# A two-layer network on one Trainium2 core: other orders of work at the opening of the state-space part

## The chip, the cores and the metric

The kernel runs on one core of one Trainium2 chip. Its time is the device time of one execution in microseconds (us). Five engines work side by side, each through its own queue in order: TensorE (PE) multiplies and transposes, ScalarE (ACT) applies functions and copies, VectorE (DVE) does elementwise arithmetic, GpSimd (POOL) does some more of it, and SyncE (SP) issues the DMA loads. They wait for each other by semaphores only.

## What is computed

The reference applies six blocks, each on a layer normalisation of `x` (4 x 256 tokens of width 512) and each added to it. The fifth is the state-space block (Mamba 2, 128 heads of 64, 8 groups, chunks of 128 tokens), whose opening is changed:

```python
proj = hidden_states @ in_proj_w.T
gate, xBC, dt = jnp.split(proj, [INTER, INTER + CONV_DIM], axis=-1)
# causal convolution of width 4 over xBC, then silu; split into x, Bm, Cm
dt = jnp.clip(jax.nn.softplus(dt + dt_bias), DT_MIN, DT_MAX)
cs = jnp.cumsum(dA, axis=-1)                       # dA = dt * A, in each chunk
Lmat = jnp.where(tri, jnp.exp(seg), 0.0)           # seg = cs[l] - cs[s]
xdt = xc * dtc[..., None]
scores = jnp.einsum('bclhn,bcshn->bchls', Cc, Bc) * Lmat
Ydiag = jnp.einsum('bchls,bcshp->bclhp', scores, xdt)
# Yoff: the first chunk's state for the second; then y * silu(gate), group norm, out projection
```

## The kernel before

All products are in float32 by three passes: each operand is split into a rounded high part and the rest (`...h`, `...l`), and `product` (L1815) runs high x high, high x low, low x high, 4 matmuls of 512 columns each, 12 for a chunk. A weight tile is loaded by SyncE into `rawA` (six slots), ScalarE makes the high part (`hi_A`, L719), GpSimd the rest (`lo_A`, L576) in place of the raw tile, and only then TensorE may use it. `A0G + i` is the i-th input-projection tile of the state-space part; chunk `c` of a group is half `c % 2` (512 tokens) of tile `c // 2`. Tiles 0 and 1 give B and C, even tiles from 2 on give x, odd ones the gate. All but the gate pass through the convolution (`conv_start` and `conv_silu` on ScalarE, three `taps` on VectorE between them); the gate takes `gate_silu`.

Each engine's order at the opening is written out by hand, and these orders are what is changed. `x` is normalised tile by tile for the new block: TensorE transposes a tile (`layer_transpose`), ScalarE copies it to `xTh` (`layer_hi`, L687), VectorE makes `xTl` (`layer_lo`, L1207), which raises `ln_lo`. TensorE runs dt_product(0), chunks 2, 4 and 6 of group 0 with the transposes of tiles 4, 5, 6 and 7 between and behind them, then waits for `ln_lo` of tile 7 and runs dt_product(1), dt_transpose(0), chunk 1, sums(0), chunk 3, the transposed sums, dt_transpose(1), chunk 5, sums(1), chunk 7, and the products of B and C.

ScalarE makes `dt` in four activations for each half of the tokens (`dt_act(p, 0)` to `dt_act(p, 3)`: bias, absolute value, exponential, logarithm; a change between exponential, logarithm and silu brings a table load), copies it token-wise (`dt_tokens`, L1073), copies the running sums (`running_sums`, L1078), and later turns the loaded rows into decays: `spans` (eight activations), then `first_exp`. SyncE's `first_rows(p)` (L446) waits for running_sums(p), writes them to memory, waits for that write and loads them back, broadcast, into `eb`; behind `first_rows(0)` in its queue stands the load of tile `A0G + 5`.

On VectorE, `scale_x(v, g, p)` scales x by dt for half p of step v and `decay_off` and `decay` (L1555) multiply the decays by the products of B and C; `decay` raises `m_s`. TensorE's `y_products(v, g, p)` (the pair products of a step; each half is one) needs `m_s` and `m_xdt`. A group has four steps v; a step on TensorE is two chunks, `y_products` of both halves, further chunks, and the transposes for the next step. GpSimd's `step` begins with the `lo_A` of the tiles that the step loads, then the squares for the norm.

Of the kernel before, what the change touches and what calls it, by code (L numbers as in the profile page):

```python
# [16 lines left out]
KC = D // P  # L17
# [30 lines left out]
def build(nc, x_in, w0_in, b0_in, lb_in, wqkv_in, wo_in, fa_in, fb_in, ma_in, mb_in, dtw_in, chp_in, cst_in, out):  # L48
# [228 lines left out]
    A0G = A0M + 1  # L277
# [72 lines left out]
    def step_tiles(v, last):  # L350

        if v < TPG - 2:
            return [2 + 2 * (v + 2), 3 + 2 * (v + 2)]
        if last:
            return []
        return [NA_G + i for i in (range(4) if v == TPG - 2 else (4, 5))]
# [129 lines left out]
    def _(pool):  # L486
# [150 lines left out]
                                    ALU.pow).then_inc(m_rstd, 1)  # L637

        def step(v, g, last=False, first=False):
            for i in step_tiles(v, last):  # L640
                lo_A(A0G + i, g, NA_G)
            if last and v == TPG - 2:
                for u in range(4):
                    lo_A(A0F + u)
            if v % 2 == 1:
                lo_B(B0G + v + 1, g, TPG)
                lo_B(B0G + v + 2, g, TPG)
            if v == 0 and not first:
                rstd_of(g - 1)
            if last and v == TPG - 2:  # L650
                pool.wait_ge(m_s, 2 * NG * TPG)
            square(v, g, 0)
            square(v, g, 1)
# [32 lines left out]
    def _(act):  # L686
        def layer_hi(k, t, bank):  # L687
            act.wait_ge(ln_tp, 8 * k + t + 1)
            nc.scalar.activation(xTh[:, :, t * P:(t + 1) * P], ps[:, bank, :].rearrange("p (k t) -> p k t", k=KC),  # L689
                                 ACT.Copy).then_inc(ln_hi, 1)  # L690
# [225 lines left out]
        def conv_start(g, c, slot):  # L916

            n = conv_index(g, c)
            act.wait_ge(m_in, chunk_count(g, c))
            if n >= 6:  # L920
                act.wait_ge(m_conv, n - 1)
            elif n == 5:
                act.wait_ge(ln_tp, 40)
            nc.scalar.activation(conv_acc(g, c), ps[:, chunk_bank(g, c), :], ACT.Identity,  # L924
                                 bias=param(slot, c // 2, 4),
                                 scale=param(slot, c // 2, 3)).then_inc(m_acc, 1)
# [190 lines left out]
        dt_act(0, 2)  # L1117
        conv_start(0, 2, 1)
        layer_hi(4, 6, 4)
        layer_hi(4, 7, 5)  # L1120
        dt_act(0, 3)
        conv_start(0, 4, 1)
        hi_B(B0G)
        hi_B(B0G + 1)
# [5 lines left out]
        dt_act(1, 3)  # L1130
        conv_start(0, 1, 1)
        conv_start(0, 3, 1)
        dt_tokens(1)
        token_sums(0)
        conv_silu(0, 0)
# [14 lines left out]
        first_exp(0)  # L1150
        spans(0, 0, 1)
        first_exp(1)
        hi_A(A0G + 5)
        act.wait_ge(m_csf, 2)
        nc.scalar.activation(erow[:, :, :], csf[:, 1:NT:2, :], ACT.Exp).then_inc(m_erow, 1)
        act.sem_inc(m_par, 4)
# [15 lines left out]
    def _(dve):  # L1172
# [615 lines left out]
        end_weights(1)  # L1788
        dve.wait_ge(m_wdt, 2)
        scale_x(0, 0, 0)  # L1790
        scale_x(0, 0, 1)
        decay_off(0, 0, 0)
        decay(0, 0, 0)
        decay_off(0, 0, 1)
        decay(0, 0, 1)
        step(0, 0, first=True)
# [14 lines left out]
    def _(pe):  # L1811
        def mm(o, l, r, start, end, **kw):
            return nc.tensor.matmul(o, l, r, start=start, stop=end, **kw)  # L1813

        def product(o, lh, ll, rh, rl, start=True, end=True, **kw):  # L1815

            passes = [(a, b) for l, r in ((lh, rh), (lh, rl), (ll, rh)) for a, b in zip(l, r)]
            for n, (a, b) in enumerate(passes):
                last = mm(o, a, b, start and n == 0, end and n == len(passes) - 1, **kw)
            return last  # L1820

# [332 lines left out]
                                       m % NF == 0, m % NF == NF - 1)  # L2154
                    last.then_inc(m_out, 1)

        def in_chunk(g, c):

            tile, half = c // 2, c % 2
            n = A0G + tile  # L2160
            pe.wait_ge(A_lo, g * NA_G + n + 1)
            if g == 0 and c < 8:
                bank = chunk_bank(g, c)
                if c == 0:
                    pe.wait_ge(f_h, 2 * NF - 1)
                elif c == 2:
                    pe.wait_ge(f_g, 2 * NF)
                elif c == 6:
                    pe.wait_ge(m_dts, 1)
                elif c % 2:  # L2170
                    pe.wait_ge(ln_lo, 40)
                    pe.wait_ge(m_tap, 3 * {1: 0, 3: 1, 5: 2, 7: 3}[c] + 3)
            else:
                p = c - 3
                gp = g if p >= 0 else g - 1
                p = p % GCH
                ptile = p // 2
                if ptile < 2 or ptile % 2 == 0:
                    k = p if ptile < 2 else 4 + (ptile - 2) // 2 * 2 + p % 2
                    pe.wait_ge(m_tap, 3 * (gp * XCH + k) + 3)  # L2180
                else:
                    pe.wait_ge(m_gate, gp * 2 * TPG + (ptile - 3) // 2 * 2 + p % 2 + 1 + (g == 0 and c == 9))
            wh, wl = wA(n)
            cols = slice(512 * half, 512 * half + 512)
            return product(ps[:, chunk_bank(g, c), :], wh, wl, [xTh[:, kc, cols] for kc in range(KC)],
                           [xTl[:, kc, cols] for kc in range(KC)])

        def chunk(g, c):
            in_chunk(g, c).then_inc(m_in, 1)

        def bc(g, b):

# [199 lines left out]
        layer_transpose(4, 4, 4, False)  # L2392
        chunk(0, 4)
        layer_transpose(4, 5, 5, False)
        chunk(0, 6)
        layer_transpose(4, 6, 4, False)
        layer_transpose(4, 7, 5, False)
        pe.wait_ge(x_new, XB[4] + NT)
        pe.wait_ge(ln_lo, 40)
        dt_product(1)  # L2400
# [119 lines left out]
```

## Time and profile before

| | |
|---|---|
| median of 3 runs | 2123.57 us (2123.4 to 2125.83) |
| profiled execution | 2123.11 us, its span 2121.3 us |
| TensorE matmul busy | 2082.7 us (98%) |
| VectorE busy | 1649.1 us (78%) |
| ScalarE busy | 1432.3 us (68%) |
| GpSimd busy | 1055.2 us (50%) |
| mean granted TensorE clock | 0.998 |

The span runs from the first to the last instruction. Busy shares are means over the whole span; the stretch of the change, about 500 to 562 us, is read by itself. A timeline merges equal instructions that follow each other: "x8" behind a line says that there are eight, and its length is that of all of them. An engine's instructions overlap slightly, so that the next can start before the last has ended. The idle time in brackets is that just before the line, and behind the arrow stands what ended it.

### The profile page before, as it was taken

What the parts mean: (1) busy time and instruction counts of PE and PEld (TensorE: products, weight loads), DVE (VectorE), ACT (ScalarE), POOL (GpSimd) and SP (SyncE); (2) the same over time, 40 slices, a digit from 0 to 9 for tenths busy, and PEclk for the clock granted to TensorE, in tenths of its full rate; (3) what the DMA queues carried; (4) which work ended last, traced back from release to release, by engine and by line L of the source; (5) the groups of instructions that cost most, each with busy time, mean ns of one, the idle gap of its engine ahead of it and who ended that gap; (6) DMA issues with size and microseconds to landing.
All of it is one profiled execution on the core that took longest, in us unless ns stands there. A gap on an engine that the chain in (4) does not pass through costs nothing.

```text
span 2121.3 us, 34818 instructions
## 1 busy us (share of the span) xinstructions
PE 2082.7 (98%) x12586; PEld 1730.0 (82%) x12596; DVE 1649.1 (78%) x2675; ACT 1432.3 (68%) x3090; POOL 1055.2 (50%) x758
## 2 busy tenths in 40 slices
PE   8999999999999999999999999999999999999999
PEld 7866698888788888888888888888888888888887
DVE  7777773325889998898898999889889889998222
ACT  5498743335978777778777877777877787783332
POOL 6577545452355356354455535535445553555452
PEclk9999999999999999999999999999999999999999
DMA  3000013332433233233224323323322432232332
GB/s 139 1 1 2 1 60 95 95 90 71 139 136 124 78 121 116 83 130 140 90 90 140 131 77 111 124 79 126 139 90 90 140 137 81 102 115 60 95 95 84
DMA packets 65337, 202.53 MB, mean 95 GB/s; under 512 B 7056, under 2 KB 9104, under 8 KB 56976
## 3 DMA queue, kind: packets, MB, share of 16 engines
q1 hardware_dynamic: 65168, 200.31, 27.9%
q8 instruction: 102, 1.67, 0.3%
q14 instruction: 67, 0.55, 0.1%
HBM read 197.39 MB, written 2.88 MB: 94 GB/s over the span
## 4 chain that ended last, share of the span: by engine, by line
PE 92%; ACT 3%; DVE 3%; issue 1%; DMA 0%; POOL 0%; DVEq 0%; SPq 0%; ACTq 0%; POOLq 0%
PE ps L1813 86%; PE ps L2211 3%; PE ps L1998 2%; PE ps L1828 1%; ACT eb L961 0%; DVE bst L1187 0%; ACT xTh L689 0%; DVE xTl L1210 0%; PE ps L2266 0%; ACT pr_a L828 0%; DVE PT L1417 0%; DVE rs L1362 0%; ACT pr_b L828 0%; DMA cst<-cst_in 0%; DVE eb L1561 0%
## 5 line engine op out<-in xcount | busy, mean ns | idle before, releaser
L580 POOL TENSOR_TENSOR wAl<-rawA,wAh 128x512 fp32r<-128x512 f32 x233 | 343.8, 1490 | 362.4 <-ACT wAh L722 362.0
L1813 PE MATMUL ps<-xTh,wAh 128*128 128x512 f32 (+1 forms) x1528 | 418.8, 396 | 3.9 <-DVE xTl L1210 3.9
L1813 PE MATMUL ps<-xTl,wAh 128*128 128x512 f32 (+1 forms) x1528 | 405.8, 387 | 0.0
L1813 PE MATMUL ps<-xTh,wAl 128*128 128x512 f32 (+1 forms) x1528 | 405.3, 387 | 0.0
L1515 DVE SCALAR_TENSOR_TENSOR work<-ps,chp,work 128x510 f32<-128x510 f32 (+2 forms) x465 | 343.4, 744 | 22.7 <-ACT work L924 12.7
L1813 PEld LDWEIGHTS ps<-xTl,wAh 128*128 128x128 f32 x1528 | 285.2, 188 | 60.1
L1813 PEld LDWEIGHTS ps<-xTh,wAl 128*128 128x128 f32 x1528 | 285.3, 188 | 58.7
L586 POOL TENSOR_TENSOR wBl<-rawB,wBh 128x512 fp32r<-128x512 f32 x108 | 139.7, 1307 | 388.0 <-ACT wBh L726 388.0
L1813 PEld LDWEIGHTS ps<-xTh,wAh 128*128 128x128 f32 x1528 | 277.1, 188 | 66.4 <-issue 12.8
L961 ACT ACTIVATE eb<-eb,gc 128x128 f32<-128x128 f32 x1008 | 307.6, 392 | 0.0
L924 ACT ACTIVATE work<-ps,gpar 128x512 f32<-128x512 f32 x155 | 119.4, 771 | 128.8 <-PE ps L1813 96.9
L630 POOL TENSOR_TENSOR sqt<-gt 128x512 f32<-128x512 f32 x110 | 167.4, 1522 | 69.6 <-DVE gt L1577 55.4
L1469 DVE TENSOR_TENSOR hs<-ps,gs 128x512 f32<-128x512 f32 x44 | 30.4, 691 | 202.1 <-PE ps L1813 167.1
L1561 DVE TENSOR_TENSOR eb<-eb,cbD 128x1024 f32<-128x1024 f32 x128 | 184.1, 1477 | 0.0
L632 POOL TENSOR_TENSOR sq<-sq,sqt 128x512 f32<-128x512 f32 x110 | 178.2, 1620 | 8.6
L1813 PE MATMUL ps<-eb,xdt 128*64 128x128 f32 x2048 | 159.6, 277 | 5.0 <-DVE eb L1561 5.0
L1813 PE MATMUL ps<-wBh,yTh 128*128 128x512 f32 x512 | 162.3, 397 | 0.0
L1813 PE MATMUL ps<-wBl,yTh 128*128 128x512 f32 x512 | 159.3, 391 | 0.0
L1813 PE MATMUL ps<-wBh,yTl 128*128 128x512 f32 x512 | 159.1, 391 | 0.0
L722 ACT ACTIVATE wAh<-rawA 128x512 fp32r<-128x512 f32 x233 | 142.2, 620 | 21.0 <-DMA rawA<-fa_in 19.4
L948 ACT ACTIVATE gt<-ps 128x512 f32<-128x512 f32 x128 | 75.7, 591 | 118.4 <-PE ps L1813 118.4
L1583 DVE SCALAR_TENSOR_TENSOR yTl<-gt,chp,yTh 128x512 fp32r<-128x512 f32 x128 | 122.1, 954 | 39.3 <-ACT yTh L975 39.1
(213 smaller groups left out, 3958.6 us busy)
## 6 DMA issues: line engine op xcount, KB each, us to landing
eb<-scr_decays SPq DMA_DIRECT2D x62, 1536.0 KB, 6.5
rawA<-ma_in SPq DMA_DIRECT2D x144, 256.0 KB, 6.8
rawA<-fa_in SPq DMA_DIRECT2D x88, 256.0 KB, 2.6
rawB<-mb_in SPq DMA_DIRECT2D x64, 256.0 KB, 2.8
rawB<-fb_in SPq DMA_DIRECT2D x44, 256.0 KB, 2.6
x<-x_in SPq DMA_DIRECT2D x8, 256.0 KB, 6.3
x_out<-x SPq DMA_DIRECT2D x8, 256.0 KB, 2.7
wqraw<-wqkv_in SPq DMA_DIRECT2D x1, 1536.0 KB, 10.7
```

What stands on the lines that cost most here:

```text
L580: nc.gpsimd.tensor_tensor(wAl[:, slot, :], rawA[:, slot, :], wAh[:, slot, :].bitcast(F32), ALU.subtract).then_inc(A_lo, 1)
L586: nc.gpsimd.tensor_tensor(wBl[:, slot, :], rawB[:, slot, :], wBh[:, slot, :].bitcast(F32), ALU.subtract).then_inc(B_lo, 1)
L630: nc.gpsimd.tensor_tensor(sqt[:, :], y, y, ALU.mult).then_inc(m_sqt, 1)
L632: nc.gpsimd.tensor_tensor(sq[:, half], sq[:, half], sqt[:, :], ALU.add).then_inc(m_sq, 1)
L722: nc.scalar.activation(wAh[:, n % SLOTA, :], rawA[:, n % SLOTA, :], ACT.Copy).then_inc(A_hi, 1)
L924: nc.scalar.activation(conv_acc(g, c), ps[:, chunk_bank(g, c), :], ACT.Identity, bias=param(slot, c // 2, 4), scale=param(slot, c // 2, 3) ...
L948: nc.scalar.activation(gt[:, v % 2, 512 * (c % 2):512 * (c % 2) + 512], ps[:, chunk_bank(g, c), :], ACT.Silu).then_inc(m_gate, 1)
L961: last = nc.scalar.activation(eb[:, v % 2, h, t, :], eb[:, v % 2, h, t, :], ACT.Relu, bias=start, scale=-1.0)
L1515: nc.vector.scalar_tensor_tensor(out=acc[:, :, j:S], in0=src[:, :, 0:S - j], scalar=param(g, c // 2, 3 - j), in1=acc[:, :, j:S], op0=ALU.m ...
L1561: nc.vector.tensor_tensor(e, e, w.unsqueeze(1).to_broadcast([P, 2, 4 * P]), ALU.mult).then_inc(m_s, 1)
L1583: nc.vector.scalar_tensor_tensor(out=yTl[:, v % 2, half], in0=gt[:, v % 2, half], scalar=param(g, 2 + 2 * v, 6), in1=yTh[:, v % 2, half].b ...
L1813: return nc.tensor.matmul(o, l, r, start=start, stop=end, **kw)
```

## The change

It alters the order of work at five places and no arithmetic.

- TensorE: the transposes of tiles 6 and 7, which stood behind chunk 6, are issued inside it, ahead of its matmuls 2 and 10 (counted from 0). `product` gets an argument `between` for this.
- ScalarE: `dt_act(0, 3)`, the logarithm of the first half, moves from behind the copy of tile 7 to ahead of it.
- ScalarE: `hi_A(A0G + 5)`, the high part of tile 5, moves from behind the last `first_exp` to ahead of `dt_tokens(1)`.
- VectorE: `scale_x(0, 0, 1)` moves behind the first half's `decay_off` and `decay`.
- GpSimd: at steps 0 and 1 of group 0 it waits for both halves' decays of that step (`m_s`) before the splits.

```diff
--- before.py
+++ after.py
@@ -637,6 +637,8 @@
                                     ALU.pow).then_inc(m_rstd, 1)
 
         def step(v, g, last=False, first=False):
+            if g == 0 and v < 2:
+                pool.wait_ge(m_s, 2 * v + 2)
             for i in step_tiles(v, last):
                 lo_A(A0G + i, g, NA_G)
             if last and v == TPG - 2:
@@ -1117,8 +1119,8 @@
         dt_act(0, 2)
         conv_start(0, 2, 1)
         layer_hi(4, 6, 4)
+        dt_act(0, 3)
         layer_hi(4, 7, 5)
-        dt_act(0, 3)
         conv_start(0, 4, 1)
         hi_B(B0G)
         hi_B(B0G + 1)
@@ -1130,6 +1132,7 @@
         dt_act(1, 3)
         conv_start(0, 1, 1)
         conv_start(0, 3, 1)
+        hi_A(A0G + 5)
         dt_tokens(1)
         token_sums(0)
         conv_silu(0, 0)
@@ -1150,7 +1153,6 @@
         first_exp(0)
         spans(0, 0, 1)
         first_exp(1)
-        hi_A(A0G + 5)
         act.wait_ge(m_csf, 2)
         nc.scalar.activation(erow[:, :, :], csf[:, 1:NT:2, :], ACT.Exp).then_inc(m_erow, 1)
         act.sem_inc(m_par, 4)
@@ -1788,9 +1790,9 @@
         end_weights(1)
         dve.wait_ge(m_wdt, 2)
         scale_x(0, 0, 0)
-        scale_x(0, 0, 1)
         decay_off(0, 0, 0)
         decay(0, 0, 0)
+        scale_x(0, 0, 1)
         decay_off(0, 0, 1)
         decay(0, 0, 1)
         step(0, 0, first=True)
@@ -1812,10 +1814,12 @@
         def mm(o, l, r, start, end, **kw):
             return nc.tensor.matmul(o, l, r, start=start, stop=end, **kw)
 
-        def product(o, lh, ll, rh, rl, start=True, end=True, **kw):
+        def product(o, lh, ll, rh, rl, start=True, end=True, between={}, **kw):
 
             passes = [(a, b) for l, r in ((lh, rh), (lh, rl), (ll, rh)) for a, b in zip(l, r)]
             for n, (a, b) in enumerate(passes):
+                if n in between:
+                    between[n]()
                 last = mm(o, a, b, start and n == 0, end and n == len(passes) - 1, **kw)
             return last
 
@@ -2154,7 +2158,7 @@
                                        m % NF == 0, m % NF == NF - 1)
                     last.then_inc(m_out, 1)
 
-        def in_chunk(g, c):
+        def in_chunk(g, c, between={}):
 
             tile, half = c // 2, c % 2
             n = A0G + tile
@@ -2183,10 +2187,10 @@
             wh, wl = wA(n)
             cols = slice(512 * half, 512 * half + 512)
             return product(ps[:, chunk_bank(g, c), :], wh, wl, [xTh[:, kc, cols] for kc in range(KC)],
-                           [xTl[:, kc, cols] for kc in range(KC)])
-
-        def chunk(g, c):
-            in_chunk(g, c).then_inc(m_in, 1)
+                           [xTl[:, kc, cols] for kc in range(KC)], between=between)
+
+        def chunk(g, c, between={}):
+            in_chunk(g, c, between).then_inc(m_in, 1)
 
         def bc(g, b):
 
@@ -2392,9 +2396,7 @@
         layer_transpose(4, 4, 4, False)
         chunk(0, 4)
         layer_transpose(4, 5, 5, False)
-        chunk(0, 6)
-        layer_transpose(4, 6, 4, False)
-        layer_transpose(4, 7, 5, False)
+        chunk(0, 6, {2: lambda: layer_transpose(4, 6, 4, False), 10: lambda: layer_transpose(4, 7, 5, False)})
         pe.wait_ge(x_new, XB[4] + NT)
         pe.wait_ge(ln_lo, 40)
         dt_product(1)
```

## Rows read from the trace of the kernel before

**Rows 1.** The page, part 1, first line: busy us (share of span) xinstructions.
```profile
PE 2082.7 (98%) x12586; PEld 1730.0 (82%) x12596; DVE 1649.1 (78%) x2675; ACT 1432.3 (68%) x3090; POOL 1055.2 (50%) x758
```

**Rows 2.** Chain that ended last, 499 to 572 us: start us, length us, what.
```profile
509.15 1.30 DVE xTl L1210 x2
...
540.57 0.52 ACT wAh L722
...
558.62 3.37 DVE eb L1561 x2
...
562.03 7.22 PE ps L1813 x48
```

**Rows 3.** Waits of TensorE, whole span: us in total, times, longest us.
```profile
PE ps L1813 <- DVE eb L1561: 5.0, 4, 2.2
```

**Rows 4.** Timeline of ScalarE: start us, length us, instruction, [idle before <-releaser].
```profile
508.52 1.08 ACT L689 ACTIVATE xTh<-ps 128x512 fp32r<-128x512 f32 x2
509.62 1.28 ACT L1071 ACT_TABLE_LOAD   x1
510.91 0.63 ACT L1071 ACTIVATE dts<-dts 128x512 f32<-128x512 f32 x1
511.45 0.76 ACT L924 ACTIVATE sqt<-ps,gpar 128x512 f32<-128x512 f32 x1
...
514.03 0.60 ACT L1075 ACTIVATE dtt<-ps 128x512 f32<-128x512 f32 x1 [0.78 <-PE ps L2363]
...
520.16 1.52 ACT L924 ACTIVATE gt<-ps,gpar 128x512 f32<-128x512 f32 x2
522.25 0.60 ACT L1075 ACTIVATE dtt<-ps 128x512 f32<-128x512 f32 x1 [0.57 <-PE ps L2363]
...
529.94 0.62 ACT L1085 ACTIVATE ctok<-ps 128x512 f32<-128x512 f32 x1
```

**Rows 5.** Timeline of TensorE, 496 to 572 us, columns as in rows 4.
```profile
510.58 1.16 PE L1813 MATMUL ps<-xTh,wAh 128*128 128x512 f32 x4 [1.67 <-DVE xTl L1210]
...
539.86 0.66 PE L1813 MATMUL ps<-eb,xdt 128*64 128x128 f32 x8 [1.08 <-DVE eb L1561]
...
543.62 1.12 PE L1813 MATMUL ps<-eb,xdt 128*64 128x128 f32 x8 [2.22 <-DVE eb L1561]
...
559.81 0.66 PE L1813 MATMUL ps<-eb,xdt 128*64 128x128 f32 x8 [1.04 <-DVE eb L1561]
...
562.03 0.66 PE L1813 MATMUL ps<-eb,xdt 128*64 128x128 f32 x8 [0.69 <-DVE eb L1561]
```

**Rows 6.** Slices of 1 us: busy time and count of each engine, then granted clock.
```profile
543.00:544.00 1.00, 0.39 (x4) 0.39 (x6) 1.00 (x2) 1.00 (x4) 1.00 (x1) 0.83 0.17 62
...
545.00:546.00 1.00, 1.00 (x12) 1.00 (x10) 0.75 (x2) 1.00 (x4) 0.00 (x0) 0.50 0.00 0
...
547.00:548.00 1.00, 1.00 (x6) 0.82 (x5) 0.93 (x3) 1.00 (x5) 1.00 (x1) 0.97 0.79 197
```

**Rows 7.** Timeline of SyncE's DMA issues: start us, length us, issue.
```profile
518.34 0.33 SPq L450 DMA_DIRECT2D scr_decays<-csf  x1
...
521.81 1.41 SPq L388 DMA_DIRECT2D rawA<-ma_in  x3
```

**Rows 8.** Line 388's landings: its issue at 521.81, then all five to 560.
```profile
DMA to landing us min/median/max: 5.2/5.2/5.2
...
DMA to landing us min/median/max: 5.2/5.5/6.9
```

**Rows 9.** The page, part 6: issue, count, KB each, median us to landing.
```profile
rawA<-fa_in SPq DMA_DIRECT2D x88, 256.0 KB, 2.6
```

**Rows 10.** Line 1561, step 0's two decays: duration ns min/median/max, start us.
```profile
L1561 DVE TENSOR_TENSOR eb<-eb,cbD x1: 1219/1219/1219, 538.6 to 538.6; 128x1024 f32<-128x1024 f32 x1
...
L1561 DVE TENSOR_TENSOR eb<-eb,cbD x1: 2289/2289/2289, 541.3 to 541.3; 128x1024 f32<-128x1024 f32 x1
```

**Rows 11.** Timeline of GpSimd, 496 to 572 us, columns as in rows 4.
```profile
541.17 3.52 POOL L580 TENSOR_TENSOR wAl<-rawA,wAh 128x512 fp32r<-128x512 f32 x2 [25.81 <-ACT wAh L722]
```

## The prediction

> **What bounds the kernel now.** I read four views in this order. The page's totals say that TensorE is busy for 98% of the span [rows 1], so the kernel is TensorE-bound almost everywhere and an edit pays or costs only where TensorE stands idle. The chain that ended last, read between 499 and 572 us, shows where that is: up to 505 us and again from 562.03 us the chain is TensorE's own, and between the two it runs mostly through ScalarE, with pieces of VectorE and one of TensorE from 510.58 to 514 [rows 2]. The waits view of TensorE agrees: its four waits for VectorE's decays, 5.0 us in all, all lie in this stretch [rows 3], and from 562.03 on it has no further one for them. So the quantity to forecast is one time stamp: when the second pair product of step 1 starts, now at 562.03 us. Whatever it shifts by, the end shifts by.
>
> The ScalarE timeline then says how full that engine is. Between 514.03 and 558 us it has one idle time of note, 0.57 us ahead of the second copy to `dtt` [rows 4]. Hence in this stretch a conversion moved from one place of ScalarE's queue to another is worth nothing by itself; every microsecond that ScalarE waits is worth a microsecond at 562. The TensorE timeline gives the idle times that are the result: 1.67 us before dt_product(1), 2.22 before the second pair product of step 0, 0.69 before the one of step 1 [rows 5].
>
> **Edit 1: the last two transposes inside chunk 6.** The same 8 transposes and 12 matmuls run, so TensorE's work is unchanged. The transposes of tile 6 now end near 506 us instead of near 508.3. Nobody uses that: ScalarE's copy of tile 6 starts at 508.52 directly behind `conv_start(0, 2)`, without idle time [rows 4]. Their own waits (`ln_norm`, `ln_lo`) are met: VectorE has nothing left before tile 6's rest but that copy. Value 0. The cover is ScalarE's queue; if it were empty, up to the 1.67 us of idle before dt_product(1) could be won.
>
> **Edit 2: dt_act(0, 3) between the copies of tiles 6 and 7.** This adds something to the path. Now the two copies take 1.08 together, then come the table load of 1.28 and the logarithm of 0.63 [rows 4]. After the edit: copy of tile 6 from 508.52 to 509.12 (a copy of this size takes 0.60, as those to `dtt`); load 509.14 to 510.42; logarithm from 510.43; the copy of tile 7 can start 0.54 after it (the pitch of the next instruction behind the logarithm at 510.91, whose neighbour starts at 511.45), so 510.97 to 511.57. VectorE's rest of tile 7 now starts at 509.75 (the pair takes 1.30 from 509.15 [rows 2], the last 0.69 of it is tile 7's); it will start at 511.59. That is +1.84, and dt_product(1), now at 510.58 [rows 5], waits for exactly this. Behind it in TensorE's queue stands dt_transpose(0), and on that waits dt_tokens(0), for which ScalarE already idles 0.78 us now [rows 4]. So that idle time grows to 2.62 us and all of ScalarE's later stream moves by **+1.84**. What is won, the logarithm 0.48 earlier, feeds dt_clip(0), which on VectorE stands behind the rest of tile 7 anyway. The Trainium skill, page "ScalarE: Activation LUTs", section "What ACT_TABLE_LOAD costs", adds about 1.38 us of drain to each switch of set; by it the copy of tile 7 would be later still and the term +3.2. The row shows the logarithm 0.01 us behind the 1.28 us load, so the trace does not agree and I keep its number.
>
> **TensorE's clock.** TensorE's idle time before dt_product(1) becomes 1.67 + 1.84 = 3.5 us. The nearest rows: after idle times of 1.08 and 2.22 us, with about 1.5 us of work between, the granted clock is 0.83 in the slice from 543 us, 0.50 (1.2 instead of 2.4 GHz) in those up to 547 and 0.97 in the next, and the first 8 matmuls take 1.12 where the same take 0.66 at full clock; behind the 1.67 us before dt_product(1) the first four take 1.16, which is full speed [rows 5, 6]. The slices hold 0.17 + 3 + 0.03 = 3.3 to 3.4 us at half clock in all, which costs half of it, 1.7 us. The new idle time is longer than the one that was followed by the lower clock, so I take **+1.70**; the ends are 0 and 1.70. It falls on dt_product(1) and dt_transpose(0), which ScalarE waits for, so nothing covers it.
>
> **Edit 3: hi_A(A0G + 5) behind conv_start(0, 3).** This is the large term. ScalarE ends the two `conv_start` at 521.68 [rows 4] and would then wait for the load of that tile. SyncE issues this load behind `first_rows(0)`: the write of the running sums at 518.34, its completion, three broadcasts, and then, at 521.81, the tile [rows 7]. The issue itself comes after ScalarE has arrived. The load lands 5.2 us later [rows 8], at 527.0. Both ends hang on running_sums(0), so edit 2 moves both alike and the gap stays. In ScalarE's queue behind the waiting conversion stand dt_tokens(1), token_sums(0), the convolution's activations and running_sums(1): all that the critical stretch consists of. The conversion starts at 527.05 and takes 0.52 of the queue, so dt_tokens(1) starts at 527.57 instead of 522.25: **+5.32** (the idle 0.57 is thereby used up). TensorE's sums(1) wait for this through VectorE. TensorE then stands about 4 us idle; should its clock fall there too, chunk 7 and its transposes end 7.65 us after dt_tokens(1), and ScalarE wants them 7.69 after (now 529.94 less 522.25 [rows 4]). It just fits: 0, with an upper end of +1.7.
> Bounds of the landing: the five loads of this line in the stretch take 5.2 to 6.9 us, the same size in the SwiGLU stage 2.6 by the page's median [rows 8, 9]. I take 5.2, the very load. The Trainium skill, page "DMA: Bandwidth & Descriptors", section "Anatomy of one DMA — SWDGE (gpsimd) path", gives 2.0 us plus the bytes over 436 GB/s, 2.6 us for 256 KB; by it the term would be +2.7 and the sum 5.0. The section is about another issuing path, and the row disagrees.
> At its old place the conversion is gone: `erow` and all that follows it on ScalarE come 0.52 earlier (its piece of the chain is 0.52 long [rows 2]): **-0.52**.
>
> **Edit 4: the decays ahead of the second scaling.** Decay 0 of step 0 no longer waits for scale_x(0, 0, 1), some 0.93 us, which moves into VectorE's idle time before the second half (it waits for the exponentials till 540.57). The first pair product of step 0 comes up to 0.9 earlier, and this is worth nothing: the second one and ScalarE's stream set what follows. If that idle time were missing, 0.93 would be lost.
>
> **Edit 5: GpSimd waits for the decays.** VectorE's decay of 128x1024 takes 1.22 us alone and 2.29 beside GpSimd's splits; the split beside it runs long as well, two splits taking 3.52 [rows 10, 11]. In step 0 the second decay ends 1.07 earlier; it feeds a pair product behind which TensorE waits again, 1.04 us at 559.81 [rows 5], so it doesn't reach 562. In step 1 the second decay is again disturbed (the two take 3.37 where 2.44 would be undisturbed [rows 2]); undisturbed it ends about 1 earlier, and the pair product starts when TensorE is free, 0.69 earlier [rows 5]: **-0.69**. The added wait queues two splits and the squares behind it on GpSimd. The splits move by 1 to 2 us, and are wanted by chunks more than 10 us away; cost 0.
>
> **Sum.** 1.84 + 1.70 + 5.32 - 0.52 - 0.69 = +7.65 us. The profiled execution took 2123.11 us (span 2121.3 and 1.8 around it), the median is 2123.57. I forecast 2130.8 for a like execution and 2131.2 for the median. A measurement of this kernel can tell about 0.2%, 4.2 us, from no change.
>
> **Rivals.**
> (a) TensorE's clock stays up over 3.5 us of idle time. For it: it stayed at 1.00 over 1.67 us. Sum 5.95, 2129.5. Chance 0.17.
> (b) The second idle time brings a lower clock that isn't covered (the margin is 0.04 us): 7.65 + 1.7, 2132.9. Chance 0.11.
> (c) The load lands in 2.6 us as in the SwiGLU stage: 5.05, 2128.6; with (a) 3.35, 2126.9, which counts as no change. Chance 0.09.
> (d) The other side: ScalarE doesn't wait at the moved conversion, because the tile is there. Then its 0.52 fits into the idle 0.57, and 1.84 + 1.70 - 1.21 = +2.3 is left, 2125.9: no change. The point from which it decides is a wait below 1.9 us, a landing by 523.6. Against it: the issue stands at 521.81 and hangs on the same queue. Chance 0.06.
> (e) As (d), and the logarithm's place costs nothing either: only -1.21 is left, 2122.4. Against it: no idle time lies between the copies. Chance 0.03.
> The forecast has 0.54.
>
> **Range.** (a) and the forecast span 5.95 to 7.65; (b) and the upper landing of 6.9 reach 9.35, with the spread of the runs before (up to 2.3 over the median) 2134; (c) reaches down to 2127. So 2127.0 to 2134.0. Slower by over 0.2%: forecast, (a), (b) and most of (c), 0.88; within: 0.11; faster 0.01.
>
> **What would show it.** Right: a ScalarE idle time of about 5.3 us ended by a DMA into `rawA` behind the second `conv_start` to `gt`; the idle time before the first `dtt` at 2.6 or 4.3 us; TensorE idle 3.5 us before dt_product(1), with a granted clock of 0.50 behind it; decays of 1.22 us; the second pair product of step 1 at 569.7. Wrong: the conversion without idle time, or dt_product(1) at 510.6; or TensorE with new idle time behind 570 us, for a split of step 1 that comes too late.

## The result

The changed kernel takes 2134.2 us (median of 6 runs, 2131.54 to 2135.98); the kernel before, beside it, 2123.55. The ratio is 1.0046, with a 95% interval of 1.0036 to 1.0056: slower, clear of noise. In a later set of runs beside the kernel before it took 2131.28 (5 runs, 2130.56 to 2134.99) against 2123.46, a ratio of 1.0038 (1.0025 to 1.0052). The forecast was 2131.2 and slower; the first median lies 0.2 us above the upper end of the stated range (2134.0), the second inside it, and the first ratio times the median before, 2133.3, too. The profiled execution took 2131.54 us with a span of 2129.4, 8.1 us more than before.

Busy times are those of before: TensorE 2083.5 us of matmuls, ScalarE 1432.0, VectorE 1648.6, GpSimd 1053.3. The loss is for the most part idle time of TensorE, and all of it stands in the opening. ScalarE's timeline of the changed kernel (columns as in rows 4):

```profile
508.43 0.59 ACT L691 ACTIVATE xTh<-ps 128x512 fp32r<-128x512 f32 x1
509.04 1.28 ACT L1073 ACT_TABLE_LOAD   x1
510.33 0.63 ACT L1073 ACTIVATE dts<-dts 128x512 f32<-128x512 f32 x1
510.87 0.58 ACT L691 ACTIVATE xTh<-ps 128x512 fp32r<-128x512 f32 x1
...
517.37 0.60 ACT L1077 ACTIVATE dtt<-ps 128x512 f32<-128x512 f32 x1 [4.21 <-PE ps L2367]
...
523.49 1.51 ACT L926 ACTIVATE gt<-ps,gpar 128x512 f32<-128x512 f32 x2
530.74 0.63 ACT L724 ACTIVATE wAh<-rawA 128x512 fp32r<-128x512 f32 x1 [5.75 <-DMA rawA<-ma_in]
531.27 0.58 ACT L1077 ACTIVATE dtt<-ps 128x512 f32<-128x512 f32 x1
...
539.74 0.60 ACT L1087 ACTIVATE ctok<-ps 128x512 f32<-128x512 f32 x1 [0.61 <-PE ps L2389]
```

Where [rows 4] had two copies side by side at 508.52, the table load and the logarithm stand between them now. The first copy to `dtt` has 4.21 us of idle time ahead of it (0.78 before), and the moved conversion (`wAh`) 5.75, ended by the DMA into `rawA`; the second copy to `dtt` is behind it. New is also the 0.61 ahead of `ctok`, which followed without idle time before. TensorE's timeline shows the same from its side:

```profile
505.04 0.71 PE L1815 MATMUL ps<-xTh,wAh 128*128 128x512 f32 x2
...
512.32 1.66 PE L1815 MATMUL ps<-xTh,wAh 128*128 128x512 f32 x4 [3.39 <-DVE xTl L1212]
513.77 1.91 PE L1815 MATMUL ps<-xTl,wAh 128*128 128x512 f32 x4
515.48 1.41 PE L1815 MATMUL ps<-xTh,wAl 128*128 128x512 f32 x4
...
533.31 2.07 PE L1815 MATMUL ps<-cst,dA 128*128 128x128 f32 x8 [5.03 <-DVE dA L1746]
...
569.10 0.66 PE L1815 MATMUL ps<-eb,xdt 128*64 128x128 f32 x8 [1.91 <-DVE eb L1563]
...
570.46 0.61 PE L1815 MATMUL ps<-eb,xdt 128*64 128x128 f32 x8
```

dt_product(1) starts at 512.32 behind 3.39 us of idle time (1.67 in [rows 5]), and its three passes take 1.66, 1.91 and 1.41 us, where they took 1.16, 1.07 and 1.07 before. The group at 570.46 is the second pair product of step 1 (569.10 is the first): the time stamp that the prediction followed, 562.03 before [rows 2, 5]. It now follows without idle time. The granted clock, in slices of 2 us (clock behind the counts):

```profile
509.00:511.00 2.00, 0.00 (x0) 0.00 (x0) 0.69 (x1) 1.97 (x4) 0.00 (x0) 1.00 0.00 0
...
513.00:515.00 2.00, 2.00 (x6) 1.57 (x5) 1.96 (x3) 0.15 (x1) 2.00 (x2) 0.50 0.00 0
515.00:517.00 2.00, 2.00 (x9) 1.58 (x8) 1.46 (x2) 0.00 (x0) 0.42 (x1) 0.71 0.00 0
...
533.00:535.00 2.00, 1.69 (x8) 1.69 (x9) 1.93 (x4) 1.99 (x4) 0.00 (x0) 0.56 0.00 0
```

Executions start the opening up to 1.1 us later or 0.2 earlier. So from here on the stamp is counted from the start of chunk 6 (505.05 before, 505.04 after): **56.98 us before, 65.42 after, +8.44.** What comes behind it is the same work in all kernels here. These stamps, and all stamps below, come from one profiled execution of each kernel.

### The profile page after: what moved, and what is told of

It reads as the page before. It is cut to its first block, busy times and chain, and to the rows that moved or that the text cites. A ratio compares the mean times of both kernels' runs of the same rounds, so it can differ in the third digit from the quotient of the medians.

```text
span 2129.4 us, 34830 instructions
## 1 busy us (share of the span) xinstructions
PE 2083.5 (98%) x12596; PEld 1729.5 (81%) x12596; DVE 1648.6 (77%) x2675; ACT 1432.0 (67%) x3090; POOL 1053.3 (49%) x758
## 3 DMA queue, kind: packets, MB, share of 16 engines
q8 instruction: 102, 1.67, 0.3%
## 4 chain that ended last, share of the span: by engine, by line
PE 92%; DVE 3%; ACT 3%; issue 1%; DMA 1%; SPq 0%; POOL 0%; DVEq 0%; ACTq 0%
PE ps L1815 86%; PE ps L2215 3%; PE ps L2002 2%; PE ps L1832 1%; ACT eb L963 0%; DVE bst L1189 0%; DMA lb_raw<-lb_in 0%; PE ps L2270 0%; ACT pr_a L830 0%; ACT xTh L691 0%; DVE xTl L1212 0%; DMA rawA<-ma_in 0%; DVE PT L1419 0%; DVE rs L1364 0%; ACT pr_b L830 0%
```

## The experiments

Each kernel ran beside the kernel before, whose median was 2123.42 to 2123.85 us in these sets; the ratio is to those runs, and not the quotient of two medians of the table. "Stamp" is the second pair product of step 1, counted from chunk 6; "tail" what is left of the span behind it; clock 1910 to 1940 is the mean granted clock in that stretch.

| kernel | median us | ratio to before (95%) | wait for the load | stamp | tail | clock 1910 to 1940 |
|---|---|---|---|---|---|---|
| before | 2123.57 | | none | 56.98 | 1559.3 | 0.94 |
| changed | 2134.20 | 1.0046 (1.0036 to 1.0056) | 5.75 | 65.42 | 1558.9 | 1.00 |
| changed, again | 2131.28 | 1.0038 (1.0025 to 1.0052) | 5.21 | 66.73 | 1561.0 | 0.89 |
| conversion back | 2126.18 | 1.0007 (0.9998 to 1.0016) | none | 59.47 | 1558.9 | 1.00 |
| logarithm back | 2130.28 | 1.0027 (1.0018 to 1.0037) | 5.39 | 62.60 | 1562.1 | 0.94 |
| both back | 2123.61 | 0.9997 (0.9987 to 1.0006) | none | 56.04 | 1561.1 | 0.89 |
| load first | 2126.03 | 1.0013 (1.0004 to 1.0022) | none | 58.94 | 1558.8 | 1.00 |
| load in between | 2127.09 | 1.0015 (1.0006 to 1.0024) | 1.27 | 61.25 | 1559.4 | 0.94 |
| first idle time filled | 2129.88 | 1.0030 (1.0019 to 1.0041) | 5.14 | 63.22 | 1558.9 | 1.00 |
| both idle times filled | 2131.96 | 1.0036 (1.0022 to 1.0049) | 6.63 | 65.04 | 1559.2 | 1.00 |
| GpSimd's wait alone | 2124.27 | 1.0004 (0.9995 to 1.0013) | none | 56.10 | 1559.7 | 0.94 |
| scaling order alone | 2123.69 | 0.9999 (0.9990 to 1.0008) | none | 56.98 | 1560.8 | 0.89 |
| load first, logarithm back | 2122.51 | 0.9992 (0.9983 to 1.0001) | none | 55.52 | 1561.0 | 0.89 |
| the same, conv_start(0, 2) late | 2121.83 | 0.9993 (0.9984 to 1.0002) | none | 55.22 | 1559.4 | 0.94 |

**1. The conversion back at its old place.** The changed kernel with

```diff
-        hi_A(A0G + 5)
         dt_tokens(1)
...
         first_exp(1)
+        hi_A(A0G + 5)
```

> The changed kernel with hi_A(A0G + 5) back at its old place behind the last first_exp. Theory W (most of the loss is ScalarE waiting 5.75 us for the load of that tile, with the dt copy behind it in its queue): no ScalarE idle time ended by a DMA here; the second pair product of step 1, at 562.03 us before and 570.46 in the changed kernel, comes at 562.03 + 1.74 + 1.60 - 0.85 = 564.5 us; time about 2126. Rival (the stretch is late for another cause, the logarithm's place and the lower TensorE clock behind it, and the wait only fills time that would be idle): it stays at 569 or later, time 2131 or more.

```profile
517.75 0.60 ACT L1077 ACTIVATE dtt<-ps 128x512 f32<-128x512 f32 x1 [4.22 <-PE ps L2367]
...
525.96 0.60 ACT L1077 ACTIVATE dtt<-ps 128x512 f32<-128x512 f32 x1 [0.60 <-PE ps L2367]
```

The idle time ended by a DMA is gone (timeline of ScalarE), the 4.22 us ahead of the first `dtt` stay. The stamp is 59.47, or +2.49 over before; the theory's sum was 1.74 + 1.60 - 0.85 = 2.49. The conversion's new place, which is the wait and what hung on it, was 5.95 of the 8.44 us.

**2. The logarithm back.** The changed kernel with

```diff
-        dt_act(0, 3)
         layer_hi(4, 7, 5)
+        dt_act(0, 3)
```

> The changed kernel with dt_act(0, 3) back behind the copy of tile 7. Theory L (its place delays dt_product(1) by 1.74 us and the lower clock behind the longer idle time costs 1.60 more): dt_product(1) starts at 510.6 again, the granted clock stays at 1.00 behind it, the first copy to dtt starts at 514.0; the wait for the load stays (about 5.5 us). Second pair product of step 1 at 570.46 - 3.34 = 567.1, time 3.3 us under that of the changed kernel, about 2128 to 2131. Rival (ScalarE absorbs the logarithm, its place is free): the pair product stays at 570.4, time as the changed kernel's.

```profile
514.53 0.60 ACT L1077 ACTIVATE dtt<-ps 128x512 f32<-128x512 f32 x1 [0.77 <-PE ps L2367]
...
527.57 0.63 ACT L724 ACTIVATE wAh<-rawA 128x512 fp32r<-128x512 f32 x1 [5.39 <-DMA rawA<-ma_in]
...
537.53 0.60 ACT L1087 ACTIVATE ctok<-ps 128x512 f32<-128x512 f32 x1 [1.58 <-PE ps L2389]
```

The first `dtt` again has 0.77 us of idle time, and the clock is 1.00 from 509 to 519 us. The stamp fell by 2.82, to 62.60, not by 3.34: the idle time ahead of the second `ctok` is 1.58 us here instead of 0.61. The copy to `dtt` behind the conversion comes 3.77 us earlier here (22.46 us after chunk 6 instead of 26.23), and 0.95 of it is lost again by the second `ctok`. In this execution the mean clock from 525 to 541 us was 0.79, in that of the changed kernel 0.89. The theory holds for the part it was about (first `dtt` 8.89 us after chunk 6, 12.33 in the changed kernel, 8.98 before), and the remainder is a second place that costs.

**3. Both back.** Both edits above in one kernel.

> Both ScalarE edits undone; left are the transposes inside chunk 6, the later second scaling and GpSimd's wait for the decays. Theory: only the gain of undisturbed decays is left, the second pair product of step 1 at 561.2 to 561.4 instead of 562.03, time 2122.7 to 2123.0 against 2123.5. Rival (one of the three other edits has a cost of its own that the large terms hide, such as a late split or a late chunk 6): at 562 or later, time 2123.5 or more.

```profile
505.08 0.71 PE L1815 MATMUL ps<-xTh,wAh 128*128 128x512 f32 x2
...
559.76 0.66 PE L1815 MATMUL ps<-eb,xdt 128*64 128x128 f32 x8 [1.92 <-DVE eb L1563]
...
561.12 0.60 PE L1815 MATMUL ps<-eb,xdt 128*64 128x128 f32 x8
```

TensorE's timeline: the second pair product (561.12) follows without idle time, 56.04 after chunk 6, 0.94 before that of the kernel before. Experiment 8 accounts for 0.88 of it, and no other edit shows a cost of its own. dt_product(1) starts 5.45 us after chunk 6 instead of 5.53, so the earlier transposes are worth 0.08. The median did not move all the same (ratio 0.9997): 0.94 us is 0.04%, and in the profiled execution the clock near 1920 us was lower for longer than in that of before (0.89 against 0.94), and the tail was 1.8 longer.

**4. The load ahead of `first_rows(0)`.** The changed kernel with, on SyncE,

```diff
-        first_rows(0)
         mamba_A(5, 0)
+        first_rows(0)
```

> The changed kernel with SyncE's load of tile A0G + 5 issued ahead of first_rows(0) instead of behind it; ScalarE's order is the changed one. Theory W (the wait comes from the load's place in SyncE's queue): the load is issued as soon as dt_product(1) is done, near 517 us, lands by 522.5 even if it takes 5.6 us, and ScalarE's conversion at 525 finds it there; no idle time ended by a DMA, second pair product of step 1 at 562.03 + 3.34 - 0.54 - 0.85 = 564.0, time about 2125.5. Rival (the load is slow for its own sake or the slot comes free late): an idle time of several us is left and the time stays above 2129.

```profile
518.01 0.33 SPq L388 DMA_DIRECT2D rawA<-ma_in  x1
522.75 0.33 SPq L450 DMA_DIRECT2D scr_decays<-csf  x1
```

SyncE's timeline: the one load is issued at 518.01, 4.7 us ahead of the write of the sums. The landings view of that issue:

```profile
DMA to landing us min/median/max: 2.5/2.5/2.5
```

It took 2.5 us, and ScalarE's conversion at 525.98 followed its `conv_start` without waiting. The stamp is 58.94, +1.96 over before; the expectation's sum was 3.34 - 0.54 - 0.85 = 1.95. So the conversion's new place costs nothing once the load stands elsewhere in SyncE's queue; the stamp is even 0.53 earlier than with the conversion at its old place (59.47 in experiment 1). The 1.96 that are left are the logarithm's place and the clock behind it, less what the other edits gain.

**5. The load in between.** The changed kernel with the same load behind the completion of the write, ahead of the three broadcasts:

```diff
             sp.wait_ge(m_scr, 16 * (p + 1))
+            if p == 0:
+                mamba_A(5, 0)
...
         first_rows(0)
-        mamba_A(5, 0)
```

> The changed kernel with the load of tile A0G + 5 issued inside first_rows(0), behind the completion of the write and ahead of the three broadcast loads. Theory Q (the load takes 5.0 to 6.6 us because three broadcasts of 768 KB in all are in front of it in the same DMA queue; first in the queue it took 2.5): it is issued 3.5 us after the running sums instead of with them in front, lands 2.6 us later, and ScalarE waits 1.3 to 1.5 us instead of 5.75; the second pair product of step 1 comes 60.5 to 61.1 us after the start of chunk 6 (65.42 in the changed kernel, 56.98 before), time 2126.5 to 2128. Rival (the memory traffic of that moment makes it slow, wherever it stands): it takes 5 us again, ScalarE waits about 3.8, the pair product at 63.4.

```profile
518.48 0.60 ACT L1078 ACTIVATE dtt<-ps 128x512 f32<-128x512 f32 x1 [5.30 <-PE ps L2368]
...
527.38 0.63 ACT L725 ACTIVATE wAh<-rawA 128x512 fp32r<-128x512 f32 x1 [1.27 <-DMA rawA<-ma_in]
```

Its landing took 2.6 us, and ScalarE waited 1.27 us (timeline). So it is the place behind the broadcasts that makes it 5.0 to 6.5 us; at the same moment, ahead of them, it is short. Whether the broadcasts hold it up by their order in the queue or by the DMA engines that they occupy is not told apart. The stamp is 61.25, over the expected 60.5 to 61.1. The first `dtt` has 5.30 us of idle time ahead of it, against 4.21 in the changed kernel: 1.09 of the stamp is a longer stretch of low clock (mean 0.66 from 509 to 519 us instead of 0.83). Without it the stamp would be 60.16, now under that range, and next to the 60.21 that experiment 4 plus the wait gives (58.94 + 1.27).

**6. TensorE kept busy ahead of dt_product(1).** The changed kernel with 14 matmuls whose result is overwritten:

```diff
         pe.wait_ge(x_new, XB[4] + NT)
+        for _ in range(14):
+            mm(ps[:, 6, :], wA(A0M)[0][0], xTh[:, 0, 0:512], True, True)
         pe.wait_ge(ln_lo, 40)
```

> The changed kernel with 14 additional matmuls of 512 columns (3.2 us) that TensorE runs in its idle time ahead of dt_product(1), into a bank that dt_product(1) then overwrites. Theory C (1.60 us of the loss is TensorE's clock at half rate behind the longer idle time): granted clock 1.00 from 509 to 525 us, dt_product(1) and its transposes run at full speed, first copy to dtt at 515.8 instead of 517.37, second pair product of step 1 at 568.9 instead of 570.46; median 1 to 2 us under the changed kernel's. Rival (those 1.60 us are a cost of the wait, not of the clock, as a longer first fill): nothing moves.

```profile
509.00:513.00 4.00, 3.89 (x17) 2.90 (x17) 1.68 (x3) 3.97 (x7) 0.00 (x0) 1.00 0.00 0
513.00:517.00 4.00, 4.00 (x21) 3.27 (x21) 3.89 (x6) 1.44 (x4) 2.72 (x2) 1.00 0.00 0
```

The clock stays at 1.00 in both slices, and the first `dtt` comes 10.68 us after chunk 6 instead of 12.33 (516.25 less 505.57): -1.65. The stamp is 63.22, lower by 2.20, since the load took 0.6 less as well (wait 5.14 against 5.75). The 1.60 us were the clock, not the wait itself. The times agree but are weaker evidence: the median is 1.4 us under the later set of the changed kernel, and the intervals of the two ratios overlap.

**7. Both idle times filled.** As 6, and 21 more behind chunk 5, into bank 4, ahead of sums(1). TensorE also waits for the copy of the first running sums ahead of them (`m_csf`), which was done long before.

> As e5_warm1, and 21 more such matmuls (4.8 us) in the idle time ahead of sums(1), where TensorE waits for the second dt copy. Theory C2 (ScalarE's 0.61 us of new idle time ahead of the second token sums is chunk 7 at half clock behind 5.03 us of idle time): that idle time goes, pair product at 568.9 - 0.8 = 568.1 us, no half clock between 509 and 550, and the runs lie closer together than the changed kernel's (2131.5 to 2136.0). Rival (that idle time has another cause, VectorE's dA or the banks): it stays, and the time is e5_warm1's.

```profile
533.15 1.16 PE L1815 MATMUL ps<-cst,dA 128*128 128x128 f32 x8 [1.18 <-DVE dA L1746]
...
568.13 1.03 PE L1815 MATMUL ps<-eb,xdt 128*64 128x128 f32 x8 [1.92 <-DVE eb L1563]
...
569.37 1.07 PE L1815 MATMUL ps<-eb,xdt 128*64 128x128 f32 x8
```

ScalarE's idle time ahead of the second `ctok` is gone, and from the second `dtt` to the first pair product of step 1 it takes 37.0 us (531.1 to 568.13) instead of 37.8 (531.27 to 569.10), as expected. The stamp that the expectation named, the second pair product, comes at 570.65 nevertheless instead of 568.1, and the median is 2131.96 (2130.78 to 2132.21), 2 us over the kernel of 6. Two causes are in its trace: the wait for the load was 6.63 us, 1.49 more than in 6, and the lower clock came at about 568.3 instead, where TensorE sets the end (timeline: a group of 8 takes 1.03 and 1.07 instead of 0.66 and 0.61, and the second pair product follows the first after 2.52 us instead of 1.36). So its five runs do lie closer together, as expected, but not earlier: the mechanism was right, the forecast of the time wrong. Whether the filling itself brought about the later low clock or the slower load is open.

**8. GpSimd's wait alone, in the kernel before.**

```diff
         def step(v, g, last=False, first=False):
+            if g == 0 and v < 2:
+                pool.wait_ge(m_s, 2 * v + 2)
```

> The kernel before with only GpSimd's wait for the decays. Theory: both second decays take 1.22 us instead of 2.29 and 2.30; only step 1's is on the path: second pair product of step 1 at 56.1 to 56.3 us after the start of chunk 6 instead of 56.98, time 0.7 to 0.9 under before. Rival (the gain of the changed kernel there comes from the earlier scaling order or from TensorE's idle time): 56.98 stays.

```profile
538.45 1.22 DVE L1563 TENSOR_TENSOR eb<-eb,cbD 128x1024 f32<-128x1024 f32 x1
...
541.13 2.29 DVE L1563 TENSOR_TENSOR eb<-eb,cbD 128x1024 f32<-128x1024 f32 x1
...
558.40 2.35 DVE L1563 TENSOR_TENSOR eb<-eb,cbD 128x1024 f32<-128x1024 f32 x2
```

```profile
543.48 0.66 PE L1815 MATMUL ps<-eb,xdt 128*64 128x128 f32 x8 [2.23 <-DVE eb L1563]
```

VectorE's timeline: step 1's two decays take 2.35 (3.44 in the kernel before), and the stamp is 56.10, -0.88: all the gain of the change. Step 0's second decay still takes 2.29, since the first split, whose conversion stands at its old place here, has no wait ahead of it; it is not on the path. Against the expectation only one of the two got shorter. TensorE's timeline (the last line) has something else to say: behind 2.23 us of idle time these 8 matmuls take 0.66, full speed, where they took 1.12 behind 2.22 in the kernel before [rows 5]. The time shows no difference (1.0004, 0.9995 to 1.0013).

**9. The scaling order alone, in the kernel before.**

```diff
         scale_x(0, 0, 0)
-        scale_x(0, 0, 1)
         decay_off(0, 0, 0)
         decay(0, 0, 0)
+        scale_x(0, 0, 1)
```

> The kernel before with only scale_x(0, 0, 1) behind the first half's decays. Theory: the first pair product of step 0 starts about 0.9 us earlier, the second one and step 1's stay: 56.98 us after the start of chunk 6, time unchanged within 0.2 us. Rival (the earlier pair product lets TensorE's later chunks and so step 1 start earlier, or the longer idle time between the two pair products brings a lower clock): step 1's second pair product moves by more than 0.3 us.

```profile
538.76 0.66 PE L1813 MATMUL ps<-eb,xdt 128*64 128x128 f32 x8 [0.16 <-DVE eb L1561]
...
543.45 0.66 PE L1813 MATMUL ps<-eb,xdt 128*64 128x128 f32 x8 [3.15 <-DVE eb L1561]
...
561.86 0.66 PE L1813 MATMUL ps<-eb,xdt 128*64 128x128 f32 x8 [0.69 <-DVE eb L1561]
```

TensorE's timeline: the first pair product of step 0 comes at 538.76 and is followed by 3.15 us of idle time instead of 2.22; from there on nothing moves, the stamp is 56.98 to the hundredth.

**10. The load first and the logarithm back.** The rest as changed:

> The changed kernel with the load of tile A0G + 5 ahead of first_rows(0) and the logarithm back behind the copy of tile 7; the early conversion stays. Theory: the conversion now lies in the 0.57 us for which ScalarE waits ahead of the second copy to dtt, so it leaves the full stretch: second pair product of step 1 at 561.13 (both ScalarE edits undone) less 0.52 = 560.6, against 562.03 before; no wait for a DMA; time 2122.0 to 2122.8. Rival (the early conversion brings nothing once it no longer waits, since something else has come last by then): 561.1 as with both undone.

ScalarE's timeline, then TensorE's:

```profile
521.31 0.62 ACT L724 ACTIVATE wAh<-rawA 128x512 fp32r<-128x512 f32 x1
521.98 0.60 ACT L1077 ACTIVATE dtt<-ps 128x512 f32<-128x512 f32 x1
```

```profile
560.38 0.61 PE L1815 MATMUL ps<-eb,xdt 128*64 128x128 f32 x8
```

The stamp is 55.52, -0.52 against experiment 3 and -1.46 against before: the conversion fills idle time of ScalarE and leaves the full stretch. The median is 2122.51, ratio 0.9992 (0.9983 to 1.0001): by the stamp it is better than both kernels, by the times it can't be told from the kernel before.

**11. And the transposes made use of.** As 10, with

```diff
         dt_act(0, 2)
-        conv_start(0, 2, 1)
         layer_hi(4, 6, 4)
         layer_hi(4, 7, 5)
+        conv_start(0, 2, 1)
         dt_act(0, 3)
```

> As e9_load_log, and conv_start(0, 2) on ScalarE behind the copies of tiles 6 and 7 instead of ahead of them. Theory T (the transposes inside chunk 6 were worth nothing because ScalarE was not free for the copies): now the copies follow the transposes at once, the copy of tile 7 ends near 508.9, dt_product(1) starts at 509.8 instead of 510.5, and as ScalarE has 0.77 us of idle time ahead of the first copy to dtt, everything comes 0.7 earlier: pair product at 559.9. Rival (another wait takes over, such as dt_clip(0) behind the logarithm): no gain over e9_load_log.

```profile
508.60 0.60 ACT L691 ACTIVATE xTh<-ps 128x512 fp32r<-128x512 f32 x1 [0.16 <-PE ps L1832]
...
513.74 0.60 ACT L1077 ACTIVATE dtt<-ps 128x512 f32<-128x512 f32 x1 [0.23 <-PE ps L2367]
```

The copy of tile 7 now waits 0.16 us for its transposes (ScalarE's timeline), and dt_product(1) starts 4.93 us after chunk 6 instead of 5.44. The gain at the stamp is 0.30, not 0.7: dt_transpose(0) then waits about 0.16 us for dt_clip(0), behind the logarithm (VectorE ends it at 513.00, and the transposes start at 513.05, 1.07 us after the last pass of dt_product(1) instead of 0.91), which is the rival's mechanism for part of it. Stamp 55.22, median 2121.83, ratio 0.9993 (0.9984 to 1.0002): the lowest median and stamp of all, and still no difference that the runs can tell from none.

**12. The changed kernel again.**

> The changed kernel once more, for the spread of its time (2131.5 to 2136.0) and for a second profile. Theory S: executions differ by how long ScalarE waits for the load (5.1 to 6.6 us were seen) and by whether a stretch of half clock falls where TensorE sets the end; the wait and the granted clock of this profile, put into the sum, give its span within 0.5 us of 2129.4 plus the differences. Rival: a longer span with the same wait and the same clock.

```profile
509.00:519.00 10.00, 6.61 (x19) 5.20 (x19) 5.59 (x7) 4.56 (x8) 2.69 (x2) 0.66 0.00 0
531.00:541.00 10.00, 6.87 (x26) 5.86 (x27) 5.76 (x7) 8.36 (x15) 1.26 (x1) 0.66 0.25 93
1910.00:1940.00 30.00, 28.75 (x205) 24.20 (x204) 25.78 (x42) 15.26 (x22) 11.28 (x11) 0.89 0.12 36
```

The same slices of the first profile:

```profile
509.00:519.00 10.00, 6.68 (x24) 5.38 (x25) 6.61 (x9) 5.73 (x10) 2.71 (x2) 0.83 0.00 0
531.00:541.00 10.00, 7.69 (x34) 6.60 (x34) 6.37 (x9) 9.36 (x18) 1.27 (x1) 0.83 0.26 82
1910.00:1940.00 30.00, 28.55 (x221) 24.15 (x220) 27.74 (x47) 15.07 (x21) 10.05 (x11) 1.00 0.11 36
```

Its span is 2132.9 us, 3.5 more than the first profile's. The mean clock is 0.66 instead of 0.83 in the first two stretches and 0.89 instead of 1.00 in the third. The first `dtt` has 5.41 us of idle time ahead of it instead of 4.21, the second `ctok` 1.28 instead of 0.61, the wait for the load is 0.54 shorter, and the stamp comes at 66.73, 1.31 later; the tail is 2.0 longer, chunk 6 starts 0.2 later. Together 3.5; the two longer idle times less the shorter wait make 1.33, where the stamp moved by 1.31. So what sets this execution apart from the first is how long the clock stays low at each of three places. That this makes the whole spread of the changed kernel is not shown. Its other execution at 2135 us in this set has the same mean clock over the span, 0.995. But in the first set the runs at 2135.60 and 2135.98 have 0.997, the same as the one at 2131.93, and a difference of 0.001, the most that the rounding hides, is 2.1 us of 2130. So at least 1.6 us there have another cause, which no profile shows.

## Why the prediction was right, and where it was not

The forecast had the right sign, the right large term and a sum 0.79 us too small. Working through that sum on the profile after, with all stamps counted from chunk 6 (the measured terms are differences of successive stamps, so they add up by construction; the experiments named are what tests them):

| term | predicted | measured | by |
|---|---|---|---|
| logarithm ahead of the copy of tile 7 | +1.84 | +1.75 | dt_product(1) at 7.28 instead of 5.53; experiments 2, 3 |
| clock behind the longer idle time | +1.70 | +1.60 | first `dtt` at 12.33 instead of 8.98, less 1.75; experiment 6 |
| wait for the load | +5.32 | +5.68 | second `dtt` at 26.23 instead of 17.20, less 3.35; experiments 1, 4, 5 |
| TensorE's second idle time | 0 | +0.80 | `spans` start 9.83 later, less 9.03; experiment 7 |
| conversion gone from its old place | -0.52 | -0.54 | exponential of step 1 9.29 later |
| decays undisturbed | -0.69 | -0.85 | stamp 8.44 later; experiment 8 (-0.88) |
| sum | +7.65 | +8.44 | |

**The large term** was right in mechanism, and the load took 5.6 us instead of 5.2. It was read as the duration of that very load, which it is only behind the broadcasts; the row of 2.6 us in the SwiGLU stage, taken for the lower bound, was what the load takes when it stands first (2.5 and 2.6). The estimate of 2.6 by the Trainium skill, page "DMA: Bandwidth & Descriptors", section "Anatomy of one DMA — SWDGE (gpsimd) path", agrees with the load that stands first, and not with the one behind the broadcasts. The drain of about 1.38 us that the page "ScalarE: Activation LUTs" of the Trainium skill, section "What ACT_TABLE_LOAD costs", adds to a table load didn't show in the changed kernel either: its logarithm starts at 510.33, 0.01 us behind the load.

**The step that failed** is "It just fits: 0". Rival (b) came true in part, at 0.80 us. The prediction set TensorE's lower clock against a margin of 0.04 us, and overlooked a second thing: the moved conversion brings its GpSimd split along, and that split now runs beside VectorE's `dA`. VectorE's and GpSimd's timelines of the changed kernel:

```profile
531.89 1.37 DVE L1746 TENSOR_TENSOR dA<-dtt,cst 128x512 f32<-128x512 f32 x1 [4.90 <-ACT dtt L1077]
```

```profile
531.45 1.27 POOL L580 TENSOR_TENSOR wAl<-rawA,wAh 128x512 fp32r<-128x512 f32 x1 [16.03 <-ACT wAh L724]
```

`dA` takes 1.37 us instead of 0.68, so sums(1) start 2.04 us after the second `dtt` instead of 1.35. The other kernels bear the cause out: in all six profiles where the split starts just ahead of the second `dA` it takes 1.37 to 1.39 us, and in all others 0.68. What a moved step brings with it includes the instruction that another engine runs because of it. It is the same contention that edit 5 removes elsewhere. In experiments 5 and 7 `dA` is as slow (1.39 and 1.38), but the clock is up, and the idle time is gone: the slow `dA` alone fits. That the low clock alone would nearly have fitted is worked out from the rows (`ctok` comes 0.78 us later behind `dtt` than before, 8.47 instead of 7.69, and 0.69 of it is `dA`), and no run has it alone.

**The clock term** has the size of its nearest row, and in part that was luck. The row was one execution: behind the same idle time, 2.23 us, the clock stayed up in experiment 8, and behind 3.15 in experiments 3 and 9. Where it did fall behind dt_product(1)'s wait, it cost 1.60 in three profiles and 2.7 to 2.8 in two, over the upper end of 1.70 that the prediction gave. Its working has a slip too: 0.17 + 3 + 0.03 is 3.2 and not 3.3 to 3.4. But a slice of 1 us at 0.83 holds 0.34 us of half clock and one at 0.97 holds 0.06, so 3.4 us and the half of it, 1.70, are what the rows say.

**Edits 1 and 4 at nothing** were right to 0.1 us: experiment 9 gives 0.00, and edit 1 shows as 0.08 or 0.09 us gained, not lost. The copy of tile 6 starts 3.39 us after chunk 6 instead of 3.47, which is also why the first term is 1.75 and not 1.84. Experiment 11 shows the cover that was named, ScalarE's queue: with it removed, the transposes' place is used and 0.5 us is won at dt_product(1).

**Edit 5**: the mechanism as said; its size was read from TensorE's idle time (0.69) where the two pair products are 1.36 apart and 0.86 was to be had. No late split showed: by the waits view TensorE waits for VectorE's decays twice, 3.8 us in all, both in the opening, and for GpSimd's splits never.

**The range** doesn't follow from its own parts at the upper end: (b) or the late landing gives +9.35 each, 2132.9, and the 2.3 us of spread make 2135.2 of it, not 2134. The first median, 2134.2, lies between the two. The range was also made from one value of each clock term. In the second profile the low clock lasted about twice as long at both places of the opening, and there was a stretch of it from 1928 us on where the first profile has none: 1.31 us at the stamp and 2.0 in the tail. Neither was among its cases. Whether the runs of the first set had the same is not shown. That the later median, 2131.28, lies 0.1 us from the forecast of 2131.2 is luck: the two medians of this kernel are 2.9 us apart, and the sum was 0.79 too small.

## What to carry to other kernels

Before a conversion is moved up in an engine's queue, look at when its load is issued and what stands ahead of it in the issuing queue; the consumer's position and the load's must move together, and here moving the load as well turned a loss of 5.95 us at the stamp into a gain of 0.53. On an engine that is full in a stretch, its order was worth nothing except where it waits or makes another wait: a table load with its function (1.9 us) put ahead of a copy that TensorE needed cost 1.75 us, and 1.60 or more again in clock. A moved step brings its followers on other engines with it, so ask what each of them will run beside.

## What the runs showed of the hardware

- The same load of 256 KB took 2.5 or 2.6 us ahead of three broadcasts of 768 KB in all (four profiles), and 5.0 to 6.5 us behind them (ten), in the same stretch.
- Behind 3.39 us of TensorE idle time the granted clock was at half in all five profiles with that idle time unfilled; the mean from 509 to 519 us was 0.83 in three and 0.66 in two, which cost 1.6 and 2.7 to 2.8 us at the first `dtt`. Behind the idle time between the pair products of step 0 it fell in the kernel before (2.22 us) and in experiment 1 (3.14), and did not in experiment 8 (2.23) and in 3 and 9 (3.15 each), so the length of the idle time alone did not decide it there.
- Where the squares are summed by matmuls of one column (from 1917 us in the kernel before, 1927 in the second profile of the changed one), the clock fell in some executions and not in others. The tail went with the mean clock from 1910 to 1940: 1558.8 to 1559.2 us at 1.00, 1559.3 to 1559.7 at 0.94, 1560.8 to 1561.1 at 0.89, with one exception, 1562.1 at 0.94, that I can't explain.
- VectorE's `dA` (128x512) took 0.68 us alone and 1.37 to 1.39 beside GpSimd's split, its decay (128x1024) 1.22 alone and 2.29 beside it.
